# Three gelus behind one table load, and three query projections in one PSUM bank

## The reference

```python
x = _L0_xattn_ref(x, ctx_1024, mask, ...)   # a Mamba-2 block, then 8-head cross-attention
x = _L1_xattn_ref(x, ctx_1024, ctx_1024, ...)  # 8 heads, then a feed-forward layer
x = _L2_xattn_ref(x, ctx_1024, ...)         # 16 heads of 16, gelu on the output
x = _L3_xattn_ref(x, ctx_1024, ...)         # 8 heads of 32, then a scan over the rows
```

```python
# layer 2
ctx = einsum('bhqk,bhkd->bhqd', softmax(scores), V)
out = q + gelu(ctx.reshape(B, N_q, 256) @ Wo + bo)        # exact gelu
# layer 3, first lines
x = _layernorm(out, g1, beta1)
q = heads(x, Wq, bq)                                       # the queries of layer 3
# layer 3, last lines: a recurrence over the 512 rows
s = silu(s @ A.T) + u_t
```

## Time and profile before

| what | us |
|---|---|
| median of three runs | 1515.5 |
| lowest and highest | 1513.93 and 1517.46 |
| the profiled execution, its time | 1517.49 |
| its span, first instruction to last | 1515.9 |
| attention loop, first quad to last | about 343 to 1407 |

### The profile page before, as it was taken

How to read it: one execution, slowest core, us unless ns; L and a number is a source line. 1 busy time by engine, 2 the same in 40 slices (tenths; PEclk the granted TensorE clock), 3 DMA queues, 4 the chain that set the end, 5 groups by cost and what they waited for, 6 DMA issues and landing times.

```text
span 1515.9 us, 35932 instructions
## 1 busy us (share of the span) xinstructions
PE 1346.9 (89%) x13436; PEld 1002.6 (66%) x13436; DVE 1039.8 (69%) x2323; ACT 1065.2 (70%) x3212; POOL 82.9 (5%) x145
## 2 busy tenths in 40 slices
PE   7999899988998889999888999988899999788855
PEld 6788666665675556777666677766676777566644
DVE  4676757756787778687777777877776787777400
ACT  4556677757788887777787677777866777787422
POOL 2000111110000000000000000000000000000000
PEclk9999999999999999999999999999999999999855
DMA  8222310012221122121101211201121121110100
GB/s 296 85 87 98 103 56 2 1 46 95 58 85 42 44 75 68 42 71 57 57 30 57 83 31 58 85 29 54 47 70 43 43 85 57 29 50 9 43 0 14
DMA packets 69883, 90.42 MB, mean 60 GB/s; under 512 B 5520, under 2 KB 58896, under 8 KB 69328
## 3 DMA queue, kind: packets, MB, share of 16 engines
q1 hardware_dynamic: 69600, 87.87, 18.2%
q0 software_dynamic: 112, 0.26, 0.1%
HBM read 71.33 MB, written 16.78 MB: 58 GB/s over the span
## 4 chain that ended last, share of the span: by engine, by line
PE 60%; DVE 14%; ACT 14%; issue 10%; POOL 0%; DMA 0%; ACTq 0%; DVEq 0%; SPq 0%; POOLq 0%
PE ps L1320 14%; PE ps L1694 11%; PE ps L1327 8%; PE ps L1334 7%; PE ps L1723 6%; ACT arena L790 5%; DVE arena L1269 5%; PE ps L1768 3%; PE ps L1397 2%; PE ps L1521 2%; PE ps L1538 2%; PE ps L1677 2%; DVE arena L949 2%; ACT R L850 1%; DVE nmax L1252 1%
## 5 line engine op out<-in xcount | busy, mean ns | idle before, releaser
L1320 PE MATMUL ps<-W,arena 128*128 128x128 f32 x2896 | 434.6, 284 | 22.3 <-ACT arena L790 19.8
L1320 PEld LDWEIGHTS ps<-W,arena 128*128 128x128 f32 x2896 | 324.9, 145 | 171.5 <-issue 129.5
L790 ACT ACTIVATE arena<-ps,nmax 128x512 f32<-128x512 f32 x640 | 435.1, 686 | 0.2
L797 ACT COPY arena<-ps 128x512 f32<-128x512 f32 x320 | 187.3, 585 | 213.0 <-PE ps L1320 208.9
L1249 DVE TENSOR_REDUCE nmax<-ps 128x1 f32<-128x512 f32 x320 | 206.1, 686 | 119.5 <-PE ps L1694 83.3
L1269 DVE COPY arena<-ps 128x512 f32<-128x512 f32 x320 | 213.8, 686 | 23.7 <-PE ps L1320 13.5
L1694 PE MATMUL ps<-W,arena 32*128 32x512 f32 x1280 | 185.2, 646 | 35.3 <-DVE arena L1269 34.2
L1723 PE MATMUL ps<-arena 128*32 128x128 f32 x5120 | 173.4, 276 | 31.6 <-ACT arena L797 31.4
L1252 DVE TENSOR_REDUCE nmax<-ps 128x2 f32<-128x1024 f32 x160 | 193.7, 1210 | 0.0
L1723 PEld LDWEIGHTS ps<-arena 128*32 128x32 f32 x5120 | 130.4, 110 | 69.5 <-ACT arena L797 59.1
L790 ACT ACTIVATION_READ_ACCUMULATOR arena<-ps,nmax 128x1 f32 x640 | 131.1, 205 | 0.0
(11 more groups left out here) (240 smaller groups left out, 1648.0 us busy)
## 6 DMA issues: line engine op xcount, KB each, us to landing
W<-keys SPq DMA_DIRECT2D x48, 512.0 KB, 3.7
arena<-values SPq DMA_DIRECT2D x48, 512.0 KB, 5.1
keys<-W SPq DMA_DIRECT2D x16, 448.0 KB, 3.0
values<-W SPq DMA_DIRECT2D x16, 448.0 KB, 3.6
W<-keys SPq DMA_DIRECT2D x16, 256.0 KB, 2.8
arena<-values SPq DMA_DIRECT2D x16, 256.0 KB, 3.3
W<-in_pack SPq DMA_DIRECT2D x1, 3180.0 KB, 10.5
CX<-in_ctx SPq DMA_DIRECT2D x4, 512.0 KB, 11.0
```

Of the source, the lines that this page charges most:

```text
L790: nc.scalar.activation(Pr[:, a, :], ps[:, a, :], ACT.Exp, bias=nmax[:, u % 32:u % 32 + 1], accum_out=den[:, u % 32:u % 32 + 1]).then_inc(s ...
L797: nc.scalar.copy(PT[:, (4 * Q + a) % 8, :, :].rearrange("p k n -> p (k n)"), psT).then_inc(sem("u_ev_act"), 1)
L1320: ins = nc.tensor.transpose(dst[:, k * P:(k + 1) * P], src[:, k * P:(k + 1) * P], ident)
```

## The change

The gelus of the batches 0, 1 and 2 of a part are made together, at the half step `gelu=3` of batch 2, and that of batch 3 alone as before. Between a group there is no exponential, so the table is loaded once for gelu and once for exp. For this, three sets of rows before the gelu must live at the same time: `orows` gets a third tile, in a part of `W` that is no longer needed, and gelu now writes in place. What follows a gelu moves too: `stats`, `nrm`, `tp`, `xT`, `q` and `qT` of the batches 0 and 1 come 15 and 9 to 10 half steps later, those of batch 2 three to four later. The queries of the three batches go one behind the other through one bank (`query_side` is 0 for them), and through one `nrm` and one `xT`. Waits keep them apart: DVE's `nrm` of batch 1 and 2 waits for the turn of the one before, and PE's `tp` waits until ACT has copied the queries of the one before. The first turn of batches 2 and 3 in layer 2 waits for the sum of two batches earlier, no more for its queries. No computation is added or left out.

```diff
+def query_side(li, b):
+    return b % 2 if li != 2 else b // 3
...
-def after_steps(li):
+def after_steps(li, b):
     step = dict(rd=0, rdT=1, on=2, wo=2, add=3)
     step.update({0: dict(tp=3), 1: dict(f_tp=3, f_xT=4, f_h=4, bias=5, f_relu=5, f_o=5, stats=6, nrm=7, tp=7),
                  2: dict(gelu=4, stats=5, nrm=6, tp=6), 3: dict(bias=2, stats=3, nrm=4, tp=4)}[li])
+    if li == 2 and b < 3:
+        step.update(({}, {}, dict(gelu=3))[b])
+        step.update((dict(stats=20, nrm=21, tp=21), dict(stats=14, nrm=15, tp=16), dict(stats=8, nrm=9, tp=10))[b])
     tp = step["tp"]
     step.update(xT=tp + 1, q=tp + 1, qT=tp + 2, u_hT=tp + 2, u_u=tp + 2, u_out=tp + 3)
...
-        orows = [a3.take(D) for _ in range(2)]
+        orows = [a3.take(D) for _ in range(2)] + [W[:, PLAN["inw"][0]:PLAN["inw"][0] + D]]
...
-                if li == 2:
+                if li == 2 and b >= 2:
                     yield step["gelu"]
-                    act.wait_ge(sem("L2_pre"), n)
-                    nc.scalar.activation(nrm[i], orows[i], ACT.Gelu).then_inc(sem("L2_gelu"), 1)
+                    for before in ((2, 1, 0) if b == 2 else (0,)):
+                        act.wait_ge(sem("L2_pre"), n - before)
+                        rows = orows[(b - before) % 3]
+                        nc.scalar.activation(rows, rows, ACT.Gelu).then_inc(sem("L2_gelu"), 1)
...
-                    nc.vector.tensor_tensor(orows[i], X[:, D:2 * D], w("bo2"), ALU.add).then_inc(sem("L2_pre"), 1)
+                    nc.vector.tensor_tensor(orows[b % 3], X[:, D:2 * D], w("bo2"), ALU.add).then_inc(sem("L2_pre"), 1)
                     yield step["stats"]
                     dve.wait_ge(sem("L2_gelu"), n)
-                    add_more(row, row, nrm[i])
-                    yield from queries("L3", n, i, row, step)
+                    add_more(row, row, orows[b % 3])
+                    yield from queries("L3", n, query_side(li, b), row, step, ("L3_xtp", n - 1) if b in (1, 2) else None)
...
-                    if pli < 3:
+                    if li == 2 and b >= 2:
+                        pe.wait_ge(sem("L2_pre"), n - 2)
+                    elif pli < 3:
                         pe.wait_ge(sem(f"{LAYERS[pli + 1].name}_qT"), turn_side(G - 2))
...
-                    yield from queries((None, "L2", "L3")[li], LAYERS[li + 1], n, b, step)
+                    yield from queries((None, "L2", "L3")[li], LAYERS[li + 1], n, b, query_side(li, b), step,
+                                       ("L3_qT", n - 1) if li == 2 and b in (1, 2) else None)
```

More of the change, by code:

```diff
@@ L506, in chain_of @@
                     return
-                n, step = turn_side(G), after_steps(li)
+                n, step = turn_side(G), after_steps(li, b)
                 if li:
                     yield step["stats"]
-                    norm({1: "L2", 2: "L3", 3: "u"}[li], n, b % 2)
+                    norm({1: "L2", 2: "L3", 3: "u"}[li], n, query_side(li, b))
                 if li == 3 and c + 1 < NCH:
@@ L715, in evac_xT, with queries @@
                     ins.then_inc(sem(f"{name}_xT"), 1)
-            def queries(l, n, b, step):
-                i = b % 2
+            def queries(l, n, b, step, i):
                 yield step["xT"]
@@ L741, in chain_of @@
                 c, li, _ = STAGES[G]
-                l, i, n, step = LAYERS[li], b % 2, turn_side(G), after_steps(li)
+                l, i, n, step = LAYERS[li], b % 2, turn_side(G), after_steps(li, b)
                 if l.quads != 2 * (wq + 1):
@@ L753, in chain_of @@
                     ins.then_inc(sem("f_hT"), 1)
-                if li == 2:
+                if li == 2 and b >= 2:
                     yield step["gelu"]
-                    act.wait_ge(sem("L2_pre"), n)
-                    nc.scalar.activation(nrm[i], orows[i], ACT.Gelu).then_inc(sem("L2_gelu"), 1)
+                    for before in ((2, 1, 0) if b == 2 else (0,)):
+                        act.wait_ge(sem("L2_pre"), n - before)
+                        rows = orows[(b - before) % 3]
+                        nc.scalar.activation(rows, rows, ACT.Gelu).then_inc(sem("L2_gelu"), 1)
                 if li < 3:
-                    yield from queries(LAYERS[li + 1], n, b, step)
+                    yield from queries(LAYERS[li + 1], n, b, step, query_side(li, b))
                     return
@@ L774, in chain_of @@
                 if c + 1 < NCH:
-                    yield from queries(L0, n + NB, b, next_steps(NEXT, 7))
+                    yield from queries(L0, n + NB, b, next_steps(NEXT, 7), i)
             def tanh_step(c, j):
@@ L1559, in last_out, with queries @@
                 proj(bank[(NT - 1) % 2][0][:, 0:D], "outw", rooms[(NT - 1) % 2].uT, D, 4).then_inc(sem("m_out"), 1)
-            def queries(kind, l, n, b, step, freed=None):
-                i = b % 2
+            def queries(kind, l, n, b, i, step, freed=None):
                 yield step["tp"]
@@ L1627, in chain_of @@
                 if c + 1 < NCH:
-                    yield from queries("pre", L0, n + NB, b, next_steps(NEXT, 7), ("u_out", n))
+                    yield from queries("pre", L0, n + NB, b, i, next_steps(NEXT, 7), ("u_out", n))
             def preload(c):
```

## The result

| | before | after |
|---|---|---|
| median of seven runs each, us | 1516.89 | 1519.95 |
| lowest and highest | 1513.93 and 1518.57 | 1517.46 and 1523.93 |
| the profiled execution: its time, its span | 1517.49, 1515.9 | 1517.90, 1516.3 |
| loop, first quad to last, in the profiled execution | 1063.9 | 1065.0 |

The ratio of the two is 1.0034, with an interval from 1.002 to 1.0047, which is a loss of 3 to 7 us; the two medians differ by 3.1. I had forecast a gain of 3. The profiled execution of after is the second shortest of its seven, so the spans of the two traces differ by 0.4 us only and the loops by 1.1; what makes the difference is in them nevertheless. In a later series one execution of the kernel before took 2120.69 us, with a mean granted clock of 0.553, and is left out of its median.

What follows compares the result with a forecast made beforehand. PE was taken as the bound, waiting in turn with ACT in each quad. Parts without new clock falls summed to -7.2 us, falls added 4.4, giving -2.8: from a median of 1515.5 to 1512.7 us, range 1506 to 1520.

Steps and rivals of the forecast that it cites:

- the term for the clock: Quad 13 or 14 of each part: one fall of TensorE's clock behind the grouped gelus, 1.1 us each, 4.4 us.
- The third pair: Earlier trace, part 2: a 9.28 us quad read as quad 14, its fall of 6.8 us at half clock priced at 1.15.
- What a gelu quad costs over a bare one: Quads 6, 10, 14 against quads without gelu or query work (5.54, 5.85 us): 1.38 us in part 0, 2.28 in part 1.
- The query pieces of quads 7 and 11: Work on the queries that leaves these quads: 0.72 us each in part 0, 0.71 in part 1.
- The group: Quad 13, between second and third exponential: two loads and three gelus, nearly all exposed, 3.6 us per part, ends 2.6 and 3.9.
- The queries: Query work and statistics packed into quads 14 to 18: 2.6 us added in part 0, 2.9 in each other part.
- Quad 15: Batch 0's `xT`, `q` and `qT` replace batch 2's `tp`, `xT` and `q`: no change in length, 0 us.
- Everything but the clock: Parts 0 to 3 without the new falls' cost: -0.4, -2.1, -2.9 and -1.8 us, together -7.2.
- The second: Rival: slower by the clock twice per part, in the group and quad 18, 1.8 us each; +6.0, 1521.5 us; chance 0.17.
- Rival 3: Quads 13 to 18: packing costs as much as grouping saves; +1.9 us, 1517.4 us, not told from no change; chance 0.13.
- Rival 1: Falls end when PE has work again, costing 0 to 0.3 us per part; -6.2 us, 1509.3 us; chance 0.2.
- The rule of the Trainium skill: TensorE: a stall of PE between bursts of work gates its clock again each time; cited against one long stall, no size.

Runs made afterwards that it cites:

- the filled kernel: Changed kernel plus 30 unused identity turns on PE while it waits for the grouped gelus, and 6 in quad 18; 1510.78 us, 0.9973 of the kernel before.
- the packed kernel: Changed kernel; without loads means Identity in place of layer 2's gelu: 1486.10 us, against 1494.01 us for the kernel before with the same edit.
- ungrouped kernels: Kernel before plus 6 identity turns per gelu quad: 1512.66 us; also late statistics for batches 0 to 2: 1506.30; also 14 turns ahead of parts 2 and 3: 1504.38.

## Why the prediction was wrong

The step that failed is the term for the clock: 4.4 us for four falls, and 2.5 us given back for those of before, where the traces show 10.9 and 4.7. Point by point, in the order of its steps:

- **A misreading first.** The third pair in the earlier trace rows is not quad 14 of part 2. Quad 6 begins there at 1011.95 us, and the row at 1038.57 is four quads on: it is quad 10 that takes 9.28 us; quad 14 takes 8.27. The sum for the part keeps its size, since one of three gelu quads is the long one either way. But the fall lay in a quad 10, and it lasted into quad 11 (6.95 us instead of 6.50), so its price was 1.6 and not 1.15.
- **What a gelu quad costs over a bare one** was right in size: quads 6 and 10 came out at 5.54 in part 0 and 5.86 in the others, and quad 14 without a fall at 5.56 and 5.85. It was wrong in what it was put down to. I called the 1.38 and 2.28 us the price of the gelu; the loads are 0.47 and 1.46 of it. For the sum that did no harm, because the statistics left these quads too. The query pieces of quads 7 and 11 were worth 0.70 us in part 0, as foreseen, but 0.52 in the others, where I had 0.71.
- **The group**: 3.6 us assumed, and quad 13 measured 9.21 at a held clock, 3.54 over its 5.67, in part 0. In the others it measured 9.91 over 5.95, 3.96.
- **The queries**: quad 16 at 6.10 and 6.42 (foreseen 6.3 and 6.5), quad 17 at 6.45 and 6.79 (6.7 and 7.1), quad 18 at 7.82 and 9.17 (7.5 and 8.8). Right in sum to 0.1 us, with quad 17 cheaper and 18 dearer. Quad 15 came to -0.1 us in part 0 and +0.2 in the others, foreseen 0.
- **Everything but the clock**: the parts came to +0.2 and three times -1.6 us, together -4.5. My terms without the falls of before (1.04, 0.34 and 1.15) say +0.6 and three times -1.8, together -4.8. Each part is within 0.5 us. That the sum is within 0.3 is luck in part: part 0 came out better than foreseen and the others worse.
- **The clock** is the step that failed. I foresaw one fall in each part, and so it came. But I took 1.1 us for a fall, 4.4 in all, from rows in which falls lasted 3.4 and 6.8 us behind two gaps of 1 us. At one gap of 3.7 to 3.9 us three of four lasted 10.2. By the difference to the filled kernel, quads 13 and 14 lost 1.3 + 2.0 us in part 0, 0.7 + 0.5 in part 1, 1.1 + 2.1 in part 2 and in part 3: 10.9 us, 2.7 each. The falls of before that went were worth 4.7 us in its profiled execution, of which I had counted 2.5. So the clock brought +6.2 net where I had +1.9, and -4.5 + 6.2 = +1.7. Measured are 1.6 us more in quads 0 to 22 of the two profiled executions and 1.1 in their loops.
- **The rivals.** The second came closest, by its place (the clock) and its price of about 1.8 for each stall, 1521.5 us. It had two falls of 6.8 us in a part; it was one, of 10.2 in three parts, and quad 18 fell in no part of the profiled execution. So it came near by a second fall that did not come. I gave it 0.17, because I scaled the fall by what I had seen and not by what had changed, the length of the stall. Rival 3, packing that costs what grouping saves, is out: without loads the packed kernel is the faster one, by 4.8 us in quads 0 to 22. Rival 1, a cheap clock, held in part 1 alone.
- The rule of the Trainium skill that I cited against the change ("TensorE: Matmul & The Clock Gate", HAM oscillation) was the one that decided. The trace agrees with it in each part: one stretch at half clock at each group, 3.4 us in part 1 and 10.2 in the others.

The ratio of the runs says 5 us where the two profiled executions differ by 0.4 in span. The mean granted clock, which is on record for each run, fits this. The seven runs of after go in order, from 1517.46 us at 0.959 to 1523.93 at 0.953, and the profiled one has 0.958 where the median has 0.956. Of before, the profiled execution has 0.961 and the median of 23 later runs, on another chip, 0.964. So a slow execution of before was profiled, and a fast one of after. What stays open is why a fall lasts 3.4 us in one part and 10.2 in the next behind gaps of the same 3.7 us, and why a kernel has more of them in one execution than in another.

## What to carry to other kernels

Ask of a costly operation where it stands before you make fewer of it: 32 loads in places half covered cost 20.0 us, and 16 in uncovered ones 20.2. A long wait of TensorE cost its own length and then a stretch at half clock, which was longer in three of four places than behind the short waits; if the wait can't be avoided, give it something to multiply. And price each piece of a crowded stretch by taking it out alone: of the 2.28 us that I called the gelu's cost in parts 1 to 3, 0.8 were the statistics of the normalization next to it.

## What was new about the hardware

- The half clock lasted 3.4 or 6.8 us behind two gaps of about 1 us, and 10.2 us in three of four parts at a gap of 3.7 to 3.9 us (3.4 in the fourth). In the kernel before the clock fell in four of the 16 gelu quads.
- Turns of the identity matrix with 1.5 to 1.7 us of idle time behind them still let the clock fall in two of four parts; with 30 of them it fell in none. With 6 turns in each of its 16 gelu quads it fell in none of them in two profiled executions of ungrouped kernels, and in two of them in a third.
- 128x128 turns that depend on nothing take 0.117 us each back to back (20 in 2.35 us).
- The attention stage began at 342.2 to 346.3 us in the 13 profiled executions, and that goes with falls ahead of all that was changed: at 342.2 to 342.8 where the half clock at about 182 us lasted 3.4 or 6.8 us, at 344.2 and 344.3 where it lasted 10.2, and at 344.4 to 346.3 where a second fall of 3.4 us, at 328 to 330 us, came on top. Differences of 2 to 4 us between single executions can come from there.
